# The output stage of a four-layer kernel: bias as a matmul, scale and shift in one ScalarE pass, loads and stores in a new order

## The chip, the core and the metric

The kernel runs on one core of one Trainium2 chip. The time is device microseconds (us) for one execution of the whole program. The engines are PE (TensorE, matmuls), DVE (VectorE), ACT (ScalarE), POOL (GpSimd) and SP (SyncE, which issues DMAs). The change touches the last stage alone, the function `phase_final`.

## The reference

The program is a stack of four layers (a recurrent mixer, a gated expert layer, a rotary attention, and a "sliced" attention), each as `x = x + layernorm(layer(layernorm(x)))` on x of shape (4, 2048, 256). The last stage does the end of the fourth layer. There `attn_out` is the attention's output, `x` the layernormed input of the layer, and each sequence of 2048 tokens is cut in 4 slices of n = 512:

```python
for e in range(e_cnt):                      # 4 slices
    sl = slice(e * n, (e + 1) * n)
    m = d // 2 ** e                         # 256, 128, 64, 32
    xm = attn_out[:, sl, :m]
    out = jnp.einsum('bnm,om->bno', xm, o_w[:m, :m]) + o_b[:m]
    pad = d - m
    if pad:
        out = jnp.pad(out, ((0, 0), (0, 0), (0, pad)))
    outs.append(out + x[:, sl, :])
...
# outside: x = x + _layernorm(that)
```

So slice e projects only the first m = 256 >> e features, adds a bias to them, adds the layer's input over the full width, takes a layernorm of the sum over 256 features, and adds the residual row.

## The kernel before, in words

`phase_final` handles 16 groups g = 4b + e of 512 tokens (b the sequence, e the slice), each as a tile of 128 partitions x 4 rows (j) x 256 features. I call groups with e = 0, 1, 2, 3 groups of **width** 256, 128, 64 and 32. What each engine does for group g:

- SP loads `AT` (attention output, transposed; 512, 256, 128 or 64 KB by width; `load_a`, L2238) into one of 3 buffers and `X` (the residual row, 512 KB; `load_x`, L2247) into one of 4. A load of X(g) waits for `y_done` of group g-4; SP's queue alternates `load_a(g)`, `load_x(g+1)`. A wait stops all that stands behind it in that queue.
- PE multiplies AT by the weights OW into PSUM tile `PA` (L2284): 8 matmuls for width 256, 4 for each other width. Each shows in the trace as two MATMUL records (x16, x8). Two PA buffers; PE waits for `z_done` of group g-2.
- DVE: `add(g)` adds the bias to PA in place (L2324), then makes Z = X * scale + PA for the first m features (L2330, 4 instructions). `stats(g)` takes mean and variance of Z (L2339, L2343). `result(g)` makes the shift NB = -mean * rs (L2350) and then Z = Z * rs + X (L2354, 4 instructions; signal `y_done`).
- POOL turns the variance into rs = (var + eps) ** -0.5 (L2269, L2272) as soon as `stats(g)` is done.
- ACT: `rest(g)` makes Z = X * scale for the features from m up (L2297, e > 0). Then `XO = Z + NB` (L2310, 4 instructions) once `y_done` and `nb_done` of the group are there, and ACT itself issues the 512 KB store (L2313).

DVE runs ahead by one group. Its program order is `add(0) stats(0)`, and then round g = `add(g+1) stats(g+1) result(g)`, for g = 0 to 15. All of this order is written out by hand; nothing is rearranged by a scheduler. ACT's order is `rest(1)`, and then `rest(g+2)`, XO(g), store(g).

Of the kernel before, what the change touches and what calls it, by code (L numbers as in the profile page):

```python
# [2203 lines left out]
def phase_final(nc, ao_d, ow_d, ob_d, scales, x_d, out_d):  # L2204
# [3 lines left out]
    NX, NZ = 4, 3  # L2208
    tag = "fin"
    with ExitStack() as ctx:  # L2210
        m = Mem(nc, ctx, tag)
        AT = [m.sb(f"AT{u}", [P, CC, GT]) for u in range(3)]
        X = [m.sb(f"X{u}", [P, J, D]) for u in range(NX)]
        Z = [m.sb(f"Z{u}", [P, J, D]) for u in range(NZ)]
        XO = [m.sb(f"XO{u}", [P, J, D]) for u in range(2)]
        OW = m.sb("OW", [P, CC, D])
        OB = m.sb("OB", [P, D])
        ST = [m.sb(f"ST{u}", [P, J, 6]) for u in range(2)]
# [17 lines left out]
        @block.sync  # L2236
        def _(sp):
            def load_a(g):  # L2238
                b, e = divmod(g, E4)
                ab = ao_d.rearrange("(b c h) d t -> b (h d) c t", b=B, c=CC)[b]  # L2240
                cs = chunks(e)
                k = cs[0][1]
                wait(sp, a_done, g - 2)
                sp.dma_start(AT[g % 3][0:k, 0:len(cs), :],
                             ab[0:k, 0:len(cs), e * GT:(e + 1) * GT]).then_inc(a_ld[g % 3], 16)

            def load_x(g):  # L2247
# [8 lines left out]
            load_x(1)
            load_x(2)
            for g in range(2, NGR):
                load_a(g)
                if g + 1 < NGR:  # L2260
                    load_x(g + 1)

        @block.gpsimd
        def _(pool):
            nc.gpsimd.memset(nhalf[:, :], -0.5).then_inc(half_set, 1)
            pool.wait_ge(half_set, 1)
            for g in range(NGR):
                wait(pool, var, g + 1)
                nc.gpsimd.tensor_scalar(VE[g % 2][:, :], MV[g % 2][:, :, 1], EPS, None, ALU.add).then_inc(eps, 1)  # L2269
                wait(pool, eps, g + 1)  # L2270
                wait(pool, nb_done, g - 1)
                nc.gpsimd.tensor_tensor(RS[g % 2][:, :], VE[g % 2][:, :], nhalf[:, :], ALU.pow).then_inc(rs, 1)  # L2272

        @block.tensor
        def _(pe):
            pe.wait_ge(ow_ld, 16)
            for g in range(NGR):
                e, u = g % E4, g % 2
                wait(pe, a_ld[g % 3], 16 * (g // 3 + 1))
                wait(pe, z_done, g - 1)  # L2280
                for j in range(J):
                    cs = chunks(e)
                    for c, k in cs:
                        ins = nc.tensor.matmul(PA[u][:, j, 0:D >> e], AT[g % 3][0:k, c, j * P:(j + 1) * P],  # L2284
                                               OW[0:k, c, 0:D >> e], start=(c == 0), stop=(c == len(cs) - 1))
                ins.then_inc(a_done, 1)

        @block.scalar
        def _(act):
# [12 lines left out]
            for g in range(NGR):  # L2302
# [15 lines left out]
        def _(dve):
            def add(g):
                u, mm = g % 2, D >> g % E4  # L2320
                if g == 0:
                    dve.wait_ge(ob_ld, 16)
                wait(dve, a_done, g + 1)
                nc.vector.tensor_tensor(PA[u][:, :, 0:mm], PA[u][:, :, 0:mm],  # L2324
                                        OB[:, 0:mm].unsqueeze(1).to_broadcast([P, J, mm]), ALU.add).then_inc(biased, 1)
                wait(dve, biased, g + 1)
# [19 lines left out]
            def result(g):  # L2346
# [13 lines left out]
            for g in range(NGR):  # L2360
# [3 lines left out]
                result(g)  # L2364
# [87 lines left out]
```

## Time and profile before

| | us |
|---|---|
| median of 3 runs | 5029.73 (5026.91 to 5038.87) |
| the profiled execution | 5029.49, of which span 5027.3 |
| last stage, first DMA issue to the end of the span | 4921.4 to 5027.3, 105.9 |
| DVE's first instruction of the stage to the end | 4931.2 to 5027.3, 96.1 |

The span is the part that the trace covers; 2.2 us of the execution lie around it. All times below count from the span's start. The page's shares of busy time (PE 92%, DVE 84%) are those of the whole program, in which an attention of some thousand us stands out. They say nothing of this stage, which is 2% of the span and is read from windows of its own.

### The profile page before, as it was taken

To read this page: it belongs to the slowest core of one execution; us is meant where nothing else is said; L and a number is where in the kernel's file an instruction comes from. 1 tells how busy PE (TensorE), PEld (TensorE's weight loads), DVE (VectorE), ACT (ScalarE), POOL (GpSimd) and SP (SyncE) were. 2 spreads that over 40 slices of the span, in tenths; PEclk is the share of its full clock that TensorE was granted. 3 is DMA by queue.
4 is the path that set the end of the run, shared out by engine and by line. 5 is a ranking of instruction groups with operands and counts; after the bars stand their busy time and mean duration, and the time that the engine had idled before them with its cause. 6 is when DMAs were issued, how large, how long until landed. Compare 5 with 4: busy or idle time off the path is not lost. (4 is left out here: it accounts for less than half of the span.)

```text
span 5027.3 us, 89365 instructions
## 1 busy us (share of the span) xinstructions
PE 4622.3 (92%) x33659; PEld 2057.7 (41%) x33659; DVE 4207.0 (84%) x5551; ACT 3361.4 (67%) x6016; POOL 1333.6 (27%) x881
## 2 busy tenths in 40 slices
PE   6998775896999999999999999999998889999993
PEld 3333541563333333333333333333334445545532
DVE  6999650787999999999999999999994777777736
ACT  4888110231888888888888888888884426666663
POOL 2333210462000000000000000000001239999992
PEclk9999887996999999999999999999997769999996
DMA  5111569687333333344333333433314831323305
GB/s 188 56 55 42 186 232 394 198 271 159 43 55 50 49 49 49 50 55 55 53 49 49 49 49 54 55 55 49 49 20 153 289 86 46 82 60 79 74 5 170
DMA packets 408176, 479.48 MB, mean 95 GB/s; under 512 B 165056, under 2 KB 311264, under 8 KB 390848
## 3 DMA queue, kind: packets, MB, share of 16 engines
q1 hardware_dynamic: 394464, 455.41, 39.2%
q10 hardware_dynamic: 13280, 18.35, 1.1%
q8 instruction: 265, 4.34, 0.4%
q14 instruction: 167, 1.37, 0.1%
HBM read 315.71 MB, written 155.58 MB: 94 GB/s over the span
## 5 line engine op out<-in xcount | busy, mean ns | idle before, releaser
L763 DVE TENSOR_REDUCE at_NM<-at_MX 128x1 f32<-128x1024 f32 (+1 forms) x3008 | 3066.3, 1049 | 241.1 <-PE at_MX L611 216.2
L715 ACT ACTIVATE at_PB<-at_S 128x512 f32<-128x512 f32 x5056 | 2712.1, 597 | 628.3 <-PE at_S L638 503.7
L611 PE MATMUL at_MX<-at_KT,at_QT 48*128 48x512 f32 (+1 forms) x5056 | 1904.2, 454 | 60.6 <-DMA at_VS<-v 46.0
L638 PE MATMUL at_S<-at_QT,at_KT 50*128 50x512 f32 (+1 forms) x5056 | 1898.6, 441 | 8.4 <-ACT at_PB L715 6.0
L650 PE MATMUL at_AV<-at_PB,at_VS 128*32 128x256 f32 (+1 forms) x18304 | 1555.5, 414 | 0.9 <-ACT at_PB L715 0.9
L638 PEld LDWEIGHTS at_S<-at_QT,at_KT 50*128 50x128 f32 (+1 forms) x5056 | 804.8, 187 | 901.1 <-ACT at_PB L715 824.8
L611 PEld LDWEIGHTS at_MX<-at_KT,at_QT 48*128 48x128 f32 (+1 forms) x5056 | 795.8, 190 | 312.5 <-DVE at_NM L763 209.5
L650 PEld LDWEIGHTS at_AV<-at_PB,at_VS 128*32 128x32 f32 x18304 | 369.8, 108 | 820.9 <-ACT at_PB L715 752.0
L547 POOL CAST at_NMR<-at_NMF 16x128 fp32r<-16x128 f32 x79 | 22.1, 279 | 1837.5 <-ACT at_NMF L727 1837.5
L572 POOL TENSOR_TENSOR at_SUM<-at_SUM,at_PB 128x2048 f32<-128x2048 f32 x90 | 415.0, 4611 | 10.9
L913 PE MATMUL wkv_PQ<-wkv_XT,wkv_WT 128*128 128x512 f32 x768 | 340.5, 600 | 50.8 <-DVE wkv_DL L1036 34.2
L572 POOL TENSOR_TENSOR at_SUM<-at_PB 128x2048 f32<-128x2048 f32 x75 | 352.2, 4699 | 30.6 <-ACT at_PB L715 30.0
L913 PEld LDWEIGHTS wkv_PQ<-wkv_XT,wkv_WT 128*128 128x128 f32 x768 | 144.7, 191 | 246.0 <-issue 194.6
L555 POOL TENSOR_TENSOR at_O<-at_FO,at_REC 128x256 f32<-128x256 f32 x64 | 39.9, 624 | 749.8 <-DVE at_REC L778 749.8
L991 POOL TENSOR_TENSOR wkv_EV<-wkv_E2S,wkv_V 128x1024 f32<-128x1024 f32 x32 | 75.5, 2360 | 311.4 <-DVE wkv_MN L1013 132.6
L1201 PE MATMUL r_PA<-r_OC,r_A 128*128 128x256 f32 x512 | 114.4, 382 | 12.3 <-DMA r_A<-ycat 12.3
L1807 PE MATMUL r_QK<-r_WC,r_XT 128*128 128x512 f32 x256 | 120.3, 594 | 0.7 <-DVE r_WC L1970 0.6
L2139 ACT ACTIVATE rows<-moe_PH 128x1024 f32<-128x1024 f32 x8 | 8.2, 1024 | 162.3 <-PE moe_TP L2181 132.0
L1488 PE MATMUL r_PO<-r_XT,r_WS 128*128 128x512 f32 (+2 forms) x136 | 92.0, 837 | 17.8 <-ACT r_XT L1517 17.8
L1201 PEld LDWEIGHTS r_PA<-r_OC,r_A 128*128 128x128 f32 x512 | 97.1, 192 | 26.7 <-DVE r_OC L1309 13.9
L727 ACT ACTIVATE at_NMF<-at_S 16x128 f32<-16x128 f32 x79 | 21.0, 266 | 120.2 <-PE at_S L629 120.2
L1885 ACT ACTIVATE r_VB<-r_PV,r_RS 128x256 f32<-128x256 f32 x64 | 26.8, 470 | 108.4 <-PE r_PV L1817 65.7
(211 smaller groups left out, 3368.0 us busy)
## 6 DMA issues: line engine op xcount, KB each, us to landing
at_QT<-qk SPq DMA_DIRECT2D x402, 128.0 KB, 5.2
moe_W<-in_w SPq DMA_DIRECT2D x48, 1024.0 KB, 11.4
at_KT<-qk SPq DMA_DIRECT2D x384, 128.0 KB, 6.5
at_VS<-v SPq DMA_DIRECT2D x96, 256.0 KB, 9.0
at_KT<-qk SPq DMA_DIRECT2D x96, 256.0 KB, 6.3
qk<-r_HI SPq DMA_DIRECT2D x36, 512.0 KB, 4.2
qk<-r_LO SPq DMA_DIRECT2D x36, 512.0 KB, 5.2
ycat<-wkv_Y SPq DMA_DIRECT2D x32, 512.0 KB, 2.6
```

The lines of the kernel that those rows point to most:

```text
L555: nc.gpsimd.tensor_tensor(O[s % 2][:, :, :], FO[s % 2][:, :, 0:DH], REC[s % 2][:, :].to_broadcast([P, W // VW, DH]), ALU.mult).then_inc(no ...
L572: nc.gpsimd.tensor_tensor(total[:, :, :], other, PB[:, k:k + NCH, :], ALU.add).then_inc(sum_done, 1)
L611: ins = nc.tensor.matmul(MX[r][:, a, :], q_of(s)[h:h + NQ, b * P:(b + 1) * P], k_of(it, s, b * P // W)[h:h + NQ, (c + a) * W:(c + a + 1) * W],
L638: nc.tensor.matmul(SP_[item(it, s, "score", t)[1]][:, :], k_of(it, s, c)[h:h + NQ + 2, kb * P:(kb + 1) * P], q_of(s)[h:h + NQ + 2, c * W:( ...
L650: ins = nc.tensor.matmul(AV[c * VW:(c + 1) * VW, cols], v_of(it, s, c)[:, kb, :], PB[:, (NCH * kb + c) % NPB, cols], start=first, stop=last)
L715: nc.scalar.activation(PB[:, t % NPB, :], SP_[r][:, :], ACT.Exp, scale=scale).then_inc(exp_done, 1)
L763: nc.vector.tensor_reduce(NM4[:, b, c:c + 1], MX[r][:, :, :].rearrange("p a n -> p (a n)"), AX_X, ALU.max, negate=True).then_inc(ring_got, 1)
L913: ins = nc.tensor.matmul(PQ[q][:, tt * 512:(tt + 1) * 512], WT[:, cc, row:row + P], XT[b % 2][:, cc, t0:t0 + 512], start=(cc == 0), stop=( ...
L991: nc.gpsimd.tensor_tensor(EV[s][:, :], E2S[s][:, :], V[s][:, :], ALU.mult).then_inc(pv, 1)
L1201: ins = nc.tensor.matmul(PA[u][:, j, :], A[u][:, q, j * P:(j + 1) * P], OC[:, q, :], start=(q == 0), stop=(q == NC - 1))
L1488: ins = nc.tensor.matmul(PO[a][:, h, :], WS[0:k, c, lo:lo + P], XT[u][0:k, c, :], start=(c == 0), stop=(c == len(ks) - 1))
L1807: ins = nc.tensor.matmul(QK[j % 2][:, :], XT[u][:, c, j * P:(j + 1) * P], WC[:, c, 0:2 * D], start=(c == 0), stop=(c == CC - 1))
```

## The change

In the last stage only:

- Bias: for widths 128, 64 and 32 PE adds it, by one more matmul for each j with a matrix ONE (row 0 ones, else zeros; two new POOL memsets) against OB. Width 256 keeps the DVE addition. PE now waits for OB's load and for ONE before its first matmul.
- Scale and shift: ACT makes XO = Z * rs + NB in its one pass; it waits for `nb_done`, no longer for `y_done`. DVE's L2354 goes. In its place DVE adds the residual row in one operation, XO = XO + X, 128 x 1024, in a new `result(g)`, which waits for `xo_done` of the group; its end is now `y_done`. The shift instruction stands in a function of its own, `shift(g)`.
- DVE's round g is now `add(g+1) stats(g+1) shift(g) result(g-1)`.
- Loads and stores: AT has 4 buffers, X 5, XO 3. SP issues A and X of groups 0 to 3 (X up to 4) at the start. Then for each g it waits for `y_done` of g and issues store(g), load X(g+5), load A(g+4), in that order. ACT issues no DMA.
- POOL's `RS` now waits for `xo_done` of group g-2, where it waited for `nb_done`.

```diff
-    NX, NZ = 4, 3
+    NA, NX, NZ, NO = 4, 5, 3, 3
...
-                wait(sp, a_done, g - 2)
-                sp.dma_start(AT[g % 3][0:k, 0:len(cs), :],
-                             ab[0:k, 0:len(cs), e * GT:(e + 1) * GT]).then_inc(a_ld[g % 3], 16)
+                wait(sp, a_done, g - NA + 1)
+                sp.dma_start(AT[g % NA][0:k, 0:len(cs), :],
+                             ab[0:k, 0:len(cs), e * GT:(e + 1) * GT]).then_inc(a_ld[g % NA], 16)
...
-            for g in range(2, NGR):
-                load_a(g)
-                if g + 1 < NGR:
-                    load_x(g + 1)
+            load_a(2)
+            load_a(3)
+            load_x(3)
+            load_x(4)
+            for g in range(NGR):
+                wait(sp, y_done, g + 1)
+                sp.dma_start(group(tokens(out_d), g), XO[g % NO][:, :, :]).then_inc(o_st[g % NO], 16)
+                if g + NX < NGR:
+                    load_x(g + NX)
+                if g + NA < NGR:
+                    load_a(g + NA)
+            for u in range(NO):
+                sp.wait_ge(o_st[u], 16 * len(range(u, NGR, NO)))
...
+            nc.gpsimd.memset(ONE[:, :], 0.0).then_inc(one_set, 1)
+            pool.wait_ge(one_set, 1)
+            nc.gpsimd.memset(ONE[0:1, :], 1.0).then_inc(one_set, 1)
...
-                wait(pool, nb_done, g - 1)
+                wait(pool, xo_done, g - 1)
...
+            pe.wait_ge(ob_ld, 16)
+            pe.wait_ge(one_set, 2)
...
-                                               OW[0:k, c, 0:D >> e], start=(c == 0), stop=(c == len(cs) - 1))
+                                               OW[0:k, c, 0:D >> e], start=(c == 0), stop=(e == 0 and c == CC - 1))
+                    if e > 0:
+                        k = cs[0][1]
+                        ins = nc.tensor.matmul(PA[u][:, j, 0:D >> e], ONE[0:k, :], OB[0:k, 0:D >> e],
+                                               start=False, stop=True)
...
-                wait(act, y_done, g + 1)
                 wait(act, nb_done, g + 1)
-                wait(act, o_st[u], 16 * (g // 2))
-                for j in range(J):
-                    ins = nc.scalar.activation(XO[u][:, j, :], Z[g % NZ][:, j, :], ACT.Identity, bias=NB[u][:, j:j + 1])
+                wait(act, o_st[g % NO], 16 * (g // NO))
+                for j in range(J):
+                    ins = nc.scalar.activation(XO[g % NO][:, j, :], Z[g % NZ][:, j, :], ACT.Identity,
+                                               bias=NB[u][:, j:j + 1], scale=RS[u][:, j:j + 1])
                 ins.then_inc(xo_done, 1)
-                wait(act, xo_done, g + 1)
-                act.dma_start(group(tokens(out_d), g), XO[u][:, :, :]).then_inc(o_st[u], 16)
...
-                wait(dve, stat, g + 1)
-                for j in range(J):
-                    ins = nc.vector.scalar_tensor_tensor(out=Z[g % NZ][:, j, :], in0=Z[g % NZ][:, j, :], scalar=RS[u][:, j:j + 1],
-                                                         in1=X[g % NX][:, j, :], op0=ALU.mult, op1=ALU.add)
-                ins.then_inc(y_done, 1)
+
+            def result(g):
+                wait(dve, xo_done, g + 1)
+                nc.vector.tensor_tensor(XO[g % NO][:, :, :], XO[g % NO][:, :, :], X[g % NX][:, :, :],
+                                        ALU.add).then_inc(y_done, 1)
...
-                result(g)
+                shift(g)
+                if g > 0:
+                    result(g - 1)
+            result(NGR - 1)
```

SP's queue in the steady part, before (X of one group, then AT of the group before it; the AT of 128x2x512 is that of a width-256 group):

```order
L2249 DMA fin_X<-x 128x1024
L2244 DMA fin_AT<-ao 64x512
L2249 DMA fin_X<-x 128x1024
L2244 DMA fin_AT<-ao 32x512
L2249 DMA fin_X<-x 128x1024
L2244 DMA fin_AT<-ao 128x2x512
```

The same queue after, from store(0) on:

```order
L2265 DMA out<-fin_XO 128x4x256
L2250 DMA fin_X<-x 128x1024
L2245 DMA fin_AT<-ao 128x2x512
L2265 DMA out<-fin_XO 128x4x256
L2250 DMA fin_X<-x 128x1024
L2245 DMA fin_AT<-ao 128x512
```

A store has moved in ahead of each pair of loads, and all three of a triple stand behind one wait for `y_done`.

DVE before, the round that ends at the bias addition of width-256 group 4 (its first row is Z of group 3, `fin_PA` with 128x1024 is group 4):

```order
L2330 SCALAR_TENSOR_TENSOR fin_Z<-fin_X,scales,fin_PA 128x32 x4
L2339 BN_STATS fin_ST<-fin_Z 128x6 x4
L2343 BN_AGGR fin_MV<-fin_ST 128x2 x4
L2350 SCALAR_TENSOR_TENSOR fin_NB<-fin_MV,fin_RS 128x4
L2354 SCALAR_TENSOR_TENSOR fin_Z<-fin_Z,fin_RS,fin_X 128x256 x4
L2324 TENSOR_TENSOR fin_PA<-fin_PA,fin_OB 128x1024
```

DVE after, from Z of group 2 to the same place (L2370 with `fin_XO` is the residual addition, first that of group 0, then that of group 1):

```order
L2345 SCALAR_TENSOR_TENSOR fin_Z<-fin_X,scales,fin_PA 128x64 x4
L2354 BN_STATS fin_ST<-fin_Z 128x6 x4
L2358 BN_AGGR fin_MV<-fin_ST 128x2 x4
L2365 SCALAR_TENSOR_TENSOR fin_NB<-fin_MV,fin_RS 128x4
L2370 TENSOR_TENSOR fin_XO<-fin_XO,fin_X 128x1024
L2345 SCALAR_TENSOR_TENSOR fin_Z<-fin_X,scales,fin_PA 128x32 x4
L2354 BN_STATS fin_ST<-fin_Z 128x6 x4
L2358 BN_AGGR fin_MV<-fin_ST 128x2 x4
L2365 SCALAR_TENSOR_TENSOR fin_NB<-fin_MV,fin_RS 128x4
L2370 TENSOR_TENSOR fin_XO<-fin_XO,fin_X 128x1024
L2339 TENSOR_TENSOR fin_PA<-fin_PA,fin_OB 128x1024
```

The instruction that signals `y_done` of a group has moved one round further down: group 0's now stands after the statistics of group 2, where it stood after those of group 1.

## Rows read from the trace of the kernel before

**Rows 1.** Busy time by window: one cycle of four groups; us, busy us by engine (records), clock, DMA.

```profile
4951.50:4974.90 23.40, 9.65 (x42) 8.22 (x41) 20.41 (x72) 12.12 (x32) 6.24 (x8) 0.64 0.72 239
```

**Rows 2.** Waits, 4918 to 5027: who waited for whom, us in total, times, longest.

```profile
PE fin_PA L2284 <- DMA fin_AT<-ao: 48.7, 8, 10.6
...
DVE fin_PA L2324 <- PE fin_PA L2284: 20.3, 4, 13.8
```

**Rows 3.** Timeline: start us, length us, engine, line, work; in brackets idle time and releaser.

```profile
4951.51 1.23 DVE L2324 TENSOR_TENSOR fin_PA<-fin_PA,fin_OB 128x1024 f32<-128x1024 f32 x1 [1.12 <-PE fin_PA L2284]
...
4957.83 0.69 DVE L2324 TENSOR_TENSOR fin_PA<-fin_PA,fin_OB 128x512 f32<-128x512 f32 x1
...
4958.56 1.12 DVE L2330 SCALAR_TENSOR_TENSOR fin_Z<-fin_X,scales,fin_PA 128x128 f32<-128x128 f32 x4
...
4961.50 1.67 DVE L2354 SCALAR_TENSOR_TENSOR fin_Z<-fin_Z,fin_RS,fin_X 128x256 f32<-128x256 f32 x4
...
4961.60 1.91 PE L2284 MATMUL fin_PA<-fin_OW,fin_AT 32*128 32x32 f32 x8 [5.95 <-DMA fin_AT<-ao]
...
4963.08 0.43 DVE L2324 TENSOR_TENSOR fin_PA<-fin_PA,fin_OB 128x256 f32<-128x256 f32 x1
4963.20 0.33 SPq L2249 DMA_DIRECT2D fin_X<-x  x1
...
4963.55 0.86 DVE L2330 SCALAR_TENSOR_TENSOR fin_Z<-fin_X,scales,fin_PA 128x64 f32<-128x64 f32 x4
4963.57 0.43 SPq L2244 DMA_DIRECT2D fin_AT<-ao  x1
...
4968.13 0.72 DVE L2330 SCALAR_TENSOR_TENSOR fin_Z<-fin_X,scales,fin_PA 128x32 f32<-128x32 f32 x4
...
4969.09 6.67 PE L2284 MATMUL fin_PA<-fin_OW,fin_AT 128*128 128x256 f32 x24 [5.58 <-DMA fin_AT<-ao]
...
4970.67 1.67 DVE L2354 SCALAR_TENSOR_TENSOR fin_Z<-fin_Z,fin_RS,fin_X 128x256 f32<-128x256 f32 x4
...
4974.90 1.23 DVE L2324 TENSOR_TENSOR fin_PA<-fin_PA,fin_OB 128x1024 f32<-128x1024 f32 x1 [2.57 <-PE fin_PA L2284]
```

**Rows 4.** Chain that ended last, shortest and longest of four width-256 PE blocks: start, us.

```profile
4925.92 5.18 PE fin_PA L2284 x16
...
4992.46 6.05 PE fin_PA L2284 x16
```

**Rows 5.** DMAs issued at 4922.4, 4941.6, 4958.3, 4963.2, 4963.6: KB, us from issue to landing.

```profile
fin_OB<-in_o_b SPq DMA_DIRECT2D x1, 128.0 KB, 5.6
...
fin_AT<-ao SPq DMA_DIRECT2D x1, 512.0 KB, 4.5
...
fin_AT<-ao SPq DMA_DIRECT2D x1, 64.0 KB, 3.3
...
fin_X<-x SPq DMA_DIRECT2D x1, 512.0 KB, 3.4
...
fin_AT<-ao SPq DMA_DIRECT2D x1, 512.0 KB, 5.5
```

**Rows 6.** PE alone by window: us, busy us (records), granted clock (1.00 is 2.4 GHz), DMA.

```profile
4961.60:4963.50 1.90, 1.90 (x8) 0.50 0.46 162
4977.90:4979.10 1.20, 1.07 (x8) 1.00 0.00 0
```

**Rows 7.** Groups of instructions, whole program: a 128x1024 addition with all operands in SBUF.

```profile
L1067 DVE TENSOR_TENSOR wkv_PD<-wkv_PD,wkv_ER 128x1024 f32<-128x1024 f32 x32 | 39.0, 1219 | 1.6 <-ACT wkv_PD L971 1.6
```

**Rows 8.** Timeline of the stage's end, same columns as rows 3.

```profile
5017.35 0.38 DVE L2343 BATCH_NORM_AGGREGATE fin_MV<-fin_ST 128x2 f32<-128x6 f32 x4
...
5018.34 1.12 POOL L2272 TENSOR_TENSOR fin_RS<-fin_VE,fin_nhalf 128x4 f32<-128x4 f32 x1
...
5021.63 1.70 ACT L2310 ACTIVATE fin_XO<-fin_Z,fin_NB 128x256 f32<-128x256 f32 x4 [0.53 <-DVE fin_Z L2354]
5023.36 0.38 ACTq L2313 DMA_DIRECT2D out<-fin_XO  x1
```

More of the change, by code:

```diff
@@ L2211, in phase_final @@
         m = Mem(nc, ctx, tag)
-        AT = [m.sb(f"AT{u}", [P, CC, GT]) for u in range(3)]
+        AT = [m.sb(f"AT{u}", [P, CC, GT]) for u in range(NA)]
         X = [m.sb(f"X{u}", [P, J, D]) for u in range(NX)]
         Z = [m.sb(f"Z{u}", [P, J, D]) for u in range(NZ)]
-        XO = [m.sb(f"XO{u}", [P, J, D]) for u in range(2)]
+        XO = [m.sb(f"XO{u}", [P, J, D]) for u in range(NO)]
         OW = m.sb("OW", [P, CC, D])
         OB = m.sb("OB", [P, D])
+        ONE = m.sb("ONE", [P, P])
         ST = [m.sb(f"ST{u}", [P, J, 6]) for u in range(2)]
@@ L2223, in phase_final @@
         PA = [m.ps(f"PA{u}", [P, J, D]) for u in range(2)]
-        ow_ld, ob_ld, half_set, a_done, biased, z_done, rest_done, stat, var, eps, rs, y_done, nb_done, xo_done = (
-            m.sem(n) for n in ("ow_ld", "ob_ld", "half_set", "a_done", "biased", "z_done", "rest_done", "stat", "var",
+        ow_ld, ob_ld, half_set, one_set, a_done, biased, z_done, rest_done, stat, var, eps, rs, y_done, nb_done, xo_done = (
+            m.sem(n) for n in ("ow_ld", "ob_ld", "half_set", "one_set", "a_done", "biased", "z_done", "rest_done", "stat", "var",
                                "eps", "rs", "y_done", "nb_done", "xo_done"))
         x_ld = [m.sem(f"x_ld{u}") for u in range(NX)]
-        a_ld = [m.sem(f"a_ld{u}") for u in range(3)]
-        o_st = [m.sem(f"o_st{u}") for u in range(2)]
+        a_ld = [m.sem(f"a_ld{u}") for u in range(NA)]
+        o_st = [m.sem(f"o_st{u}") for u in range(NO)]
         block = ctx.enter_context(nc.Block())
@@ L2276, in _ @@
             pe.wait_ge(ow_ld, 16)
+            pe.wait_ge(ob_ld, 16)
+            pe.wait_ge(one_set, 2)
             for g in range(NGR):
                 e, u = g % E4, g % 2
-                wait(pe, a_ld[g % 3], 16 * (g // 3 + 1))
+                wait(pe, a_ld[g % NA], 16 * (g // NA + 1))
                 wait(pe, z_done, g - 1)
@@ L2283, in _ @@
                     for c, k in cs:
-                        ins = nc.tensor.matmul(PA[u][:, j, 0:D >> e], AT[g % 3][0:k, c, j * P:(j + 1) * P],
-                                               OW[0:k, c, 0:D >> e], start=(c == 0), stop=(c == len(cs) - 1))
+                        ins = nc.tensor.matmul(PA[u][:, j, 0:D >> e], AT[g % NA][0:k, c, j * P:(j + 1) * P],
+                                               OW[0:k, c, 0:D >> e], start=(c == 0), stop=(e == 0 and c == CC - 1))
[3 more added lines that the diff above has]
+                                               start=False, stop=True)
                 ins.then_inc(a_done, 1)
@@ L2320, in add @@
                 u, mm = g % 2, D >> g % E4
-                if g == 0:
+                wait(dve, a_done, g + 1)
+                if mm == D:
                     dve.wait_ge(ob_ld, 16)
[L2323 to L2326, printed above, removed]
+                    nc.vector.tensor_tensor(PA[u][:, :, :], PA[u][:, :, :], OB[:, :].unsqueeze(1).to_broadcast([P, J, D]),
+                                            ALU.add).then_inc(biased, 1)
+                    wait(dve, biased, g // E4 + 1)
                 wait(dve, x_ld[g % NX], 16 * (g // NX + 1))
@@ L2344, in stats, with shift @@
                 ins.then_inc(var, 1)
-            def result(g):
+            def shift(g):
                 u = g % 2
```

2 lines of the change are left out of this document (removed).

## The prediction

> **What bounds the stage now.** I read the window of one full cycle of four groups first [rows 1]. From one width-256 bias addition to the next pass 23.40 us; DVE is busy 20.41 of them, ACT 12.12, PE 9.65, and the DMA engines 0.72 of the time at 239 GB/s. So DVE is the bound, with a remainder of about 3 us a cycle. The waits say what the remainder is: DVE waited 20.3 us for PE in four waits, the longest 13.8 being the start of the stage, so 6.5 in the other three; and PE had waited for loads of AT [rows 2]. The timeline shows one such place: AT of group 8 (width 256) is issued at 4963.57, PE starts at 4969.09, DVE idles 2.57 us until 4974.90 [rows 3]. PE, ACT and POOL idle elsewhere without cost. Of this, DVE's own work is what the change takes away; the chain "load of AT, PE, DVE" is what it moves.
>
> **DVE's work per group, before.** Start to start in [rows 3]: width 256 takes 4957.83 - 4951.51 = 6.3 us; width 128 takes 4963.08 - 4957.83 = 5.25, of which the bias addition 4958.56 - 4957.83 = 0.73; width 64 from its Z on, without the bias, is about 4.25 (the width-128 one is 4963.08 - 4958.56 = 4.5, and its four narrower Z instructions save 0.26: 1.12 against 0.86); width 32 without bias is 4970.67 - 4968.13 = 2.54, plus the L2354 block. That block occupies 4963.08 - 4961.50 = 1.58 us.
>
> **DVE's work after.** Three bias additions of four go. L2354 (1.58) goes, and one 128x1024 addition comes: 1.22 us in the row where all operands lie in SBUF [rows 7]; with the gap for its wait I take 1.25, so 0.33 saved a group. A round then is 6.0, 4.2, 3.9 and 3.8 us for widths 256, 128, 64, 32, in sum 17.9 against 23.4 with the wait or 20.7 without. ACT's pass with scale as well as bias has no row of this stage; between no change (1.70 for four [rows 8]) and double it, it stays hidden: it starts at `shift(g)` and is needed one round later, 3.8 us at the least. Cost nothing; were that cover gone, 1.7 a group. The stores' 0.38 us of issue leave ACT, which has slack. DMA bytes do not change: at 239 / 0.72 = 332 GB/s, the cycle's 5 MB need 15 us, under 17.9.
>
> **The start.** PE began at 4925.92 and took 5.18 [rows 4]. It now waits for OB too, issued at 4922.4 with 5.6 us to land [rows 5]: 4928.0, so 2.1 us later. ONE's two memsets are done by then. DVE's first instruction is at 4928.0 + 5.2 + 0.1 = 4933.3.
>
> **When is AT issued now?** This is the step that decides. A(g+4) is issued after `y_done` of g, behind store(g) and X(g+5). But `result(g)` has moved one round down, so between the end of result(0) and the bias addition of group 4 lies one round, that of group 3: 3.8 us. Before, A(g+4) was also issued at `y_done` of g (X is ahead of it in SP's queue), but that stood two rounds ahead. "Four groups ahead" by number is one round ahead in time.
>
> What must fit in that round, for width 256: the landing. A fixed part of a DMA, from a lone 512 KB: 3.4 us [rows 5] less 0.524 MB / 332 GB/s = 1.6 leaves 1.8. Store, X and A are 1.57 MB, 4.7 us, so 6.5, plus 0.1 for the semaphore: A lands 6.6 us after `y_done`. Below, it could be 5.3: X issue to A landed was 0.37 + 4.5 = 4.9 once [rows 3, 5], plus 0.4 for the store's issue if its bytes don't hold A back. Above, 7.5: the other row (0.37 + 5.5) plus 1.6 for the store. I take 6.6, between them, because the store is first in the same queue. Then PE, 5.18 to 6.05 [rows 4]; I take 5.6. Sum 6.6 + 5.6 + 0.1 = **12.3** us after `y_done`, against 3.8 of cover: DVE idles 8.5.
>
> The rows show that a load behind another in SP's queue lands later (64 KB behind X 3.3, 512 KB behind X 4.5 and 5.5 [rows 5]). The Trainium skill, page "DMA: Bandwidth & Descriptors", section "Queues, rings and completion order", says that each DMA engine consumes one issuer's descriptors in ring order and takes turns between issuers; that speaks against moving stores into SP's queue. By that rule A lands at 6.6; if the store's bytes took their turn behind it, at 5.3, and each cycle would be 1.3 us shorter.
>
> **Width 64.** A(g+4) of width 64 is issued at the end of the width-256 round and has one width-128 round, 4.2 us. Store, X and 128 KB are 1.18 MB: 3.6 + 1.8 = 5.4 us. PE now runs 8 matmuls, 16 records. PE was at full clock for 8 records in 1.07 us when it had just worked, and at 0.50 (1.2 GHz) for 8 records in 1.90 after idling 5.95 us in wait for a load [rows 3, 6]. So 16 records cost 2.1 or 3.8. Here PE has idled some 9 us (its blocks for groups 8 and 9 end about 2 us into the cycle, the AT lands at 11.4), so I take 3.8: 5.4 + 3.8 = 9.2, DVE idles 5.0 us. The Trainium skill, page "TensorE: Matmul & The Clock Gate", section "What's actually happening", says that the throttled state is the default and activity releases it; by it the block starts slow, 3.8, and without it the cycle would be 1.7 shorter. For widths 128 and 32 the extra matmuls hide: their AT was issued before the long wait, and PE does them while DVE works on the group before.
>
> **The sum.** A cycle from the width-256 addition: 6.0; 4.2; then the width-64 addition at 6.0 + 9.2 = 15.2; 3.9 on, at 19.1, `y_done` releases the next width-256 load (and width 32 starts: its AT came at 10.2 + 5.4 = 15.6, PE 2.1 to 3.8, not late by more than 0.3); next cycle at 19.1 + 12.3 = **31.4** against 23.4. First cycle: 4933.3 + 4.7 (group 0 without L2354) + 3.0 (group 1 without a result) + 3.9 = 4944.9 is result(0)'s end; group 4 starts at 4957.2, where it was at 4951.51. Two cycles: 5020.0 for group 12. Group 15 starts 19.1 later, 5039.1; its statistics end 2.6 later, 5041.7. The tail: before, 5017.73 to 5027.3, 9.6 us. After: POOL 1.73, shift 0.2, ACT 1.75, addition 1.3, store 5023.36 to 5027.3 = 3.9, in all 9.0 [rows 8]. Span 5050.7, plus 2.2 around it: **5053 us**, 23 over the profiled 5029.5, which is the median (5029.7) to 0.3 us. Most of it is the 8.0 a cycle: waits of 13.5 in place of 2.6, less 2.8 of DVE work saved.
>
> **Rivals.**
> - *The same mechanism at its low ends* (landing 5.3, PE 5.2, width 64: 4.1 + 0.1 + 2.1 = 6.3). The cycle is 6.0 + 6.3 + 3.9 + 10.6 = 26.8; group 4 at 4955.5, group 12 at 5009.1, group 15 at 5025.3, end 5036.9: 5039 us, within 0.3% of before. For it: one landing row. Against it: all ends must come together. At the high ends (7.5 + 6.05 + 0.05; width 64: 10.1) the cycle is 33.6 and the time 5059.5.
> - *DVE stays the bound* and the change gains: each AT is there in time. Then after 4944.9 come 3.8, two cycles of 17.9, and 14.1 to group 15 at 4998.6; 5001.2, end 5010.2: 5012 us, 17 faster. It needs landing and PE together within 3.8 us of `y_done`, where PE alone took 5.18 [rows 4]; or loads that don't wait for `y_done` of their triple, which the queue rules out.
> - *A wait in ACT's queue*: `rest(g+2)` stands ahead of XO(g) and waits for X(g+2), and XO(g) for store(g-3). X(g+2) is issued two rounds and a statistic ahead, over 8 us, and lands in about 5; with `rest` (1.5) and XO (1.7) it just fits. If X took 8 us, result would be late about 2 us in narrow rounds, say 10 over the stage: 5063.
>
> **How the numbers follow.** Forecast as summed, any size between 5045 and 5060: 0.73. Low ends, 5038 to 5045: 0.14; a part of the low ends and a mild clock, still within 0.3%: 0.04. DVE-bound, faster: 0.04. ACT's wait or more: 0.05. A measurement of this kernel can tell about 0.3% from no change, 15 us: slower means over 5044.8. Slower 0.78, same 0.18, faster 0.04. Range 5038 to 5062, from the low ends to just over the high ends.
>
> **What would show it.** In the new profile: PE's first matmul near 4928; DVE idle of about 8.5 us before each of three width-256 additions and about 5 before width-64 Z of groups 6, 10, 14, with PE as the releaser and the AT load ahead of it; cycles of 31; DVE busy 17 to 18 a cycle; ACT's L2328 at about 0.5 us each. Wrong would be: waits under 4 us before width 256, width-64 blocks at full clock (2.1), or a DVE addition of XO far from 1.22.

## The result

The changed kernel takes 5057.8 us in the median of 5 runs (5052.1 to 5068.9), the kernel before 5030.4 in the median of 5 (5026.9 to 5038.9). The ratio is 1.0051, 95% interval 1.0037 to 1.0065: slower by half a per cent. The forecast was 5053 with a range of 5038 to 5062.

The stage's length from its first DMA issue to the end of the span was 105.9 us before. Here the issue is at 4934.00, so it is 5067.0 - 4934.0 = **133.0 us**, 27.1 more, close to the difference of the medians (27.3). The point at which the stage starts wanders between executions by far more than the changes under study: 4913.8 to 4940.3 in all kernels below, whose earlier stages are the same code. So I compare stage lengths, not spans. A second profiled execution of the changed kernel gave 5057.2 - 4924.4 = 132.8.

First, one full cycle of four groups, from one width-256 bias addition to the next; the columns are those of [rows 1]:

```profile
4971.04:5002.30 31.26, 14.28 (x65) 12.97 (x64) 17.27 (x57) 12.66 (x28) 8.85 (x8) 0.62 0.50 166
```

DVE is busy 17.27 us of 31.3, where it was 20.41 of 23.4: the work was taken off as meant, and DVE is no longer the bound. The DMA engines' share falls from 0.72 to 0.50. PE's busy time rises from 9.65 to 14.28. What all of them wait for stands in the waits of the stage, answering to [rows 2]:

```profile
ACT fin_XO L2328 <- DVE fin_NB L2365: 63.0, 15, 11.4
...
PE fin_PA L2299 <- DMA fin_AT<-ao: 53.0, 6, 10.6
DVE fin_PA L2339 <- PE fin_PA L2299: 43.9, 4, 16.9
...
DVE fin_Z L2345 <- PE fin_PA L2303: 16.6, 3, 6.0
PE fin_PA L2299 <- DMA fin_OB<-in_o_b: 12.6, 1, 12.6
```

The longest of DVE's four waits of L2339 is the start (16.9); 27.0 lie in the other three, 9 each, where before these three had 6.5 in all. L2345 adds 16.6 in three waits, which the kernel before did not have: these are the width-64 groups, whose first instruction is now the Z instruction. The last row is PE's wait before its first matmul of the stage, which the load of OB now ends. The timeline around groups 6 to 8 answers to [rows 3]:

```profile
4977.02 0.39 SPq L2265 DMA_DIRECT2D out<-fin_XO  x1
...
4977.46 0.50 SPq L2250 DMA_DIRECT2D fin_X<-x  x1
4978.01 0.97 SPq L2245 DMA_DIRECT2D fin_AT<-ao  x1
...
4982.62 0.69 PE L2299 MATMUL fin_PA<-fin_OW,fin_AT 64*128 64x64 f32 x2 [9.84 <-DMA fin_AT<-ao]
...
4985.67 0.63 PE L2303 MATMUL fin_PA<-fin_OB,fin_ONE 64*128 64x64 f32 x2
...
4986.34 0.85 DVE L2345 SCALAR_TENSOR_TENSOR fin_Z<-fin_X,scales,fin_PA 128x64 f32<-128x64 f32 x4 [5.27 <-PE fin_PA L2303]
...
4989.01 1.22 DVE L2370 TENSOR_TENSOR fin_XO<-fin_XO,fin_X 128x1024 f32<-128x1024 f32 x1
...
4990.14 0.71 DVE L2345 SCALAR_TENSOR_TENSOR fin_Z<-fin_X,scales,fin_PA 128x32 f32<-128x32 f32 x4
4990.25 0.39 SPq L2265 DMA_DIRECT2D out<-fin_XO  x1
...
4990.69 0.50 SPq L2250 DMA_DIRECT2D fin_X<-x  x1
...
4991.24 0.95 SPq L2245 DMA_DIRECT2D fin_AT<-ao  x1
...
4992.67 1.22 DVE L2370 TENSOR_TENSOR fin_XO<-fin_XO,fin_X 128x1024 f32<-128x1024 f32 x1
...
4996.99 5.63 PE L2299 MATMUL fin_PA<-fin_OW,fin_AT 128*128 128x256 f32 x18 [7.14 <-DMA fin_AT<-ao]
...
5002.43 1.23 DVE L2339 TENSOR_TENSOR fin_PA<-fin_PA,fin_OB 128x1024 f32<-128x1024 f32 x1 [8.54 <-PE fin_PA L2299]
```

Read it from the store of group 2, issued at 4977.02: X(7) and A(6) stand behind it, and AT of group 6 (width 64) is issued at 4978.01, late because `y_done` of group 2 is. PE starts group 6 at 4982.62, 5.6 us after the store's issue, and is done at 4986.3; DVE has idled 5.27 us. From 4989.01 to 4990.23 DVE makes result(4) (L2370): this releases store(4) at 4990.25, X(9) and A(8), issued at 4991.24. Between this and the place where DVE needs group 8 (width 256) there is one DVE round, that of group 7, from 4990.14 to 4993.9. PE starts group 8 at 4996.99, 6.7 us after the store's issue, and DVE at 5002.43, after 8.54 us of idleness.

PE's clock answers to [rows 6]. The windows are the width-64 block, the start and the end of the width-256 block:

```profile
4982.62:4986.20 3.58, 3.58 (x16) 0.50 0.77 255
4996.99:4998.99 2.00, 2.00 (x5) 0.50 1.04 399
5000.40:5002.40 2.00, 2.00 (x11) 0.99 0.00 0
```

The columns are as in [rows 6]. After 9.84 us without work the 16 records of the width-64 block take 3.6 us, all at 0.50.

### The profile page after: what moved, and what is told of

It is laid out like the page before. It is cut to its first block and busy times, and to the rows that moved or that the text cites. A ratio compares the mean times of both kernels' runs of the same rounds, so it can differ in the third digit from the quotient of the medians.

```text
span 5067.0 us, 89500 instructions
## 1 busy us (share of the span) xinstructions
PE 4653.8 (92%) x33755; PEld 2082.5 (41%) x33755; DVE 4195.5 (83%) x5491; ACT 3368.5 (66%) x6016; POOL 1341.5 (26%) x883
## 5 line engine op out<-in xcount | busy, mean ns | idle before, releaser
L1201 PE MATMUL r_PA<-r_OC,r_A 128*128 128x256 f32 x512 | 117.6, 390 | 12.3 <-DMA r_A<-ycat 12.3
L2139 ACT ACTIVATE rows<-moe_PH 128x1024 f32<-128x1024 f32 x8 | 8.2, 1024 | 163.0 <-PE moe_TP L2181 131.9
L2299 PE MATMUL fin_PA<-fin_OW,fin_AT 128*128 128x256 f32 (+3 forms) x160 | 48.9, 436 | 67.8 <-DMA fin_AT<-ao 53.0
## 6 DMA issues: line engine op xcount, KB each, us to landing
moe_W<-in_w SPq DMA_DIRECT2D x48, 1024.0 KB, 11.9
```

The lines of the kernel that those rows point to most:

```text
L1201: ins = nc.tensor.matmul(PA[u][:, j, :], A[u][:, q, j * P:(j + 1) * P], OC[:, q, :], start=(q == 0), stop=(q == NC - 1))
L2299: ins = nc.tensor.matmul(PA[u][:, j, 0:D >> e], AT[g % NA][0:k, c, j * P:(j + 1) * P], OW[0:k, c, 0:D >> e], start=(c == 0), stop=(e == 0 ...
```

## The experiments

Each kernel is the changed kernel, or the one before, with the edit shown. "Stage" is always from the stage's first DMA issue to the end of the span, from one profiled execution. Of the experiments only e1 and e6 were timed more often and have an interval; the others stand on one execution, and the two kernels that were profiled twice agree with themselves to 0.3 us.

| kernel | stage | cycle(s) between width-256 additions |
|---|---|---|
| before | 105.9 | 23.4, 23.6 |
| changed | 133.0 and 132.8 | 31.4, 33.0 |
| e1, AT load ahead of the wait | 103.1 | 21.9, 25.6 |
| e2, store last | 121.7 | 28.1, 27.9 |
| e3 / e11, bias by DVE | 129.3 / 129.6 | 30.5, 30.7 / 31.1, 31.3 |
| e4, result in its own round | 125.5 | 27.1, 28.1 |
| e5, before with bias by PE | 105.5 | 21.6, 23.2 |
| e6, AT 8 ahead | 87.6 | 17.4, 17.4 |
| e7, the same, bias by DVE | 93.1 | 18.9, 18.9 |
| e8, before with AT 6 ahead | 99.9 | 20.7, 20.7 |
| e9, OB waited for later | 133.0 | 31.4, 32.9 |

### e1: release a round earlier

```diff
             for g in range(NGR):
+                if g + NA < NGR:
+                    load_a(g + NA)
                 wait(sp, y_done, g + 1)
                 sp.dma_start(group(tokens(out_d), g), XO[g % NO][:, :, :]).then_inc(o_st[g % NO], 16)
                 if g + NX < NGR:
                     load_x(g + NX)
-                if g + NA < NGR:
-                    load_a(g + NA)
```

> The changed kernel with one edit: in SP's loop load A(g+4) stands ahead of the wait for y_done of g, so it is released one round earlier (by y_done of g-1). Stage means the last stage, from its first DMA issue to the end of the span: 105.9 us before, 133.0 changed; cycles from one width-256 addition to the next are 31.4 and 33.1 in the changed kernel. Late-release theory (AT is released one DVE round before it is needed): with two rounds of cover, 7.7 us, against 12.5 needed, the wait before width 256 falls from 9 to about 4.8, that before width 64 goes, cycles of 22.5 to 23, group 4 starts 8.5 us earlier, stage about 101, time about 5025. Queue-order rival (the store ahead of the load is what costs): store and X are still ahead of the load, so nothing changes, stage about 133. PE-block rival (the doubled narrow matmul blocks cost it): stage 125 or more.

Measured: stage 103.1, and 5026.1 us in the median of 10 runs against 5033.2 of 13 of the kernel before, ratio 0.9987 (0.9977 to 0.9996). Each load but the first still has a store and an X ahead of it in the queue; it merely belongs to the `y_done` of the group before. The waits are these:

```profile
DVE fin_PA L2339 <- PE fin_PA L2299: 26.3, 4, 16.2
...
DVE fin_Z L2345 <- PE fin_PA L2303: 4.1, 3, 1.7
```

Of the 43.9 us, 26.3 are left, 16.2 of them the start; the 16.6 of width 64 are gone, and 4.1 has come for width 32, whose PE block now is the late one. The late-release theory gets its 30 us (133.0 to 103.1, 101 expected); the queue-order rival and the PE-block rival fall as explanations of the whole. The three waits before width 256 were 0.83, 2.81 and 6.39 us, in sum 10.0, the last more than expected. AT of group 12 was issued at 4980.49 and took 7.8 us to land, where that of group 8, issued at 4958.80 in the same place of its cycle, took 5.4; PE began it at 4988.28, and its block took 6.8 us, the first 6 of them at a granted clock of 0.50. The windows of those 6 us show the DMA engines busy all the time (the last two columns are their share and GB/s):

```profile
4981.00:4983.00 2.00, 1.72 (x8) 1.72 (x9) 1.97 (x9) 1.94 (x5) 0.81 (x1) 0.50 0.97 281
4983.00:4985.00 2.00, 1.90 (x9) 1.77 (x9) 0.34 (x2) 1.62 (x4) 1.41 (x2) 0.50 1.00 347
4985.00:4987.00 2.00, 0.00 (x0) 0.00 (x0) 1.97 (x8) 0.00 (x0) 0.00 (x0) 0.50 1.07 379
```

So once the release is early, what is left is partly a backlog on the DMA engines. That the bytes ahead of this load made its landing late was not tried by a kernel of its own.

### e2: same release, store behind the loads

```diff
                 wait(sp, y_done, g + 1)
-                sp.dma_start(group(tokens(out_d), g), XO[g % NO][:, :, :]).then_inc(o_st[g % NO], 16)
-                if g + NX < NGR:
-                    load_x(g + NX)
                 if g + NA < NGR:
                     load_a(g + NA)
+                if g + NX < NGR:
+                    load_x(g + NX)
+                sp.dma_start(group(tokens(out_d), g), XO[g % NO][:, :, :]).then_inc(o_st[g % NO], 16)
```

> The changed kernel with one edit: after each wait for y_done SP issues load A(g+4), load X(g+5), store(g), in that order; the release is as late as before. Queue-order effect alone: A lands about 4.0 us after y_done instead of 6.6 for width 256 and 3.2 instead of 5.4 for width 64; waits of 6.3 and 3; cycles of about 27.4; stage about 119. If the queue takes the transfers in turn and not in order, A lands as late as now and the stage stays at 132 to 133. If queue order were the whole loss, stage about 106.

Measured: stage 121.7, 11 less than the changed kernel and 3 more than expected; waits before width 256 of 8.0, 7.2 and 6.6 us, before width 64 of 3.3 to 3.7. So the order within the triple is a real part, about 2 us per wait, and the lateness of the triple as a whole is the larger part.

The traces split these 2 us. In the changed kernel AT of width 256 is issued 1.0 us after the store and lands 5.6 to 5.7 us after its own issue; here it is issued first and lands after 5.0 to 5.1. So 1.0 us is the earlier issue, and only some 0.6 the bytes of store and X. For width 64 (128 KB) the landing falls from 4.6 to 5.0 us to 3.6 to 3.9. The 4.0 us that were expected for width 256 did not come, though nothing stood ahead of the load. These are the windows behind its issue at 4973.06 (the last two columns are the DMA engines' share and GB/s):

```profile
4974.06:4975.06 1.00, 0.00 (x0) 0.00 (x0) 1.00 (x4) 0.00 (x0) 0.18 (x1) 0.50 0.84 193
4975.06:4976.06 1.00, 0.00 (x0) 0.00 (x0) 0.96 (x7) 0.46 (x1) 0.45 (x1) 0.50 0.87 137
4976.06:4977.06 1.00, 0.00 (x0) 0.00 (x0) 0.64 (x1) 1.00 (x3) 0.92 (x2) 0.50 0.82 186
4977.06:4978.06 1.00, 0.00 (x0) 0.00 (x0) 0.00 (x0) 0.62 (x2) 0.83 (x1) 0.50 0.98 374
```

The first three move 0.516 MB, as much as the AT load has (0.524), at 137 to 193 GB/s with the engines busy 0.82 to 0.87 of the time; the rate rises to 374 only behind them. AT landed at 4978.2, X at 4979.5 and the store at 4980.8, in the order of their issue. That agrees with the ring-order rule that the prediction took from the Trainium skill, page "DMA: Bandwidth & Descriptors", section "Queues, rings and completion order". No run moves the stores back to ACT's queue, so what that part of the change costs by itself is not shown.

### e3 and e11: the bias by DVE again

The edit takes out the ONE matmuls and PE's waits for OB and ONE, and puts the DVE addition back for every width:

```diff
-                    if e > 0:
-                        k = cs[0][1]
-                        ins = nc.tensor.matmul(PA[u][:, j, 0:D >> e], ONE[0:k, :], OB[0:k, 0:D >> e],
-                                               start=False, stop=True)
...
-                if mm == D:
-                    dve.wait_ge(ob_ld, 16)
-                    nc.vector.tensor_tensor(PA[u][:, :, :], PA[u][:, :, :], OB[:, :].unsqueeze(1).to_broadcast([P, J, D]),
+                nc.vector.tensor_tensor(PA[u][:, :, 0:mm], PA[u][:, :, 0:mm],
+                                        OB[:, 0:mm].unsqueeze(1).to_broadcast([P, J, mm]), ALU.add).then_inc(biased, 1)
```

> The changed kernel with the bias of all widths added by DVE again, as in the kernel before (PE no longer waits for OB and ONE; no extra matmuls). Late-release theory: the width-64 PE block falls from 3.8 to 1.9 us, DVE gains 1.45 us of work a cycle, the start is 2 us earlier: waits of about 8.5 (width 256) and 2.4 (width 64), cycles of about 30.2, stage about 126. PE-block rival: the loss is mostly here, stage 106 to 112.

> The changed kernel with the bias of all widths by DVE, once more: in the first execution group 0's AT took 5.5 us to land and its PE block 6.36, and the stage was 129.3 where 126 was expected. If that was the start's chance, the stage is 126 to 128 and the waits before widths 256 and 64 are again 8.2 and 2.4; if 129 comes again, the PE bias costs 4 us in the changed kernel and no more.

Measured: 129.3, then 129.6. So in the changed kernel the PE bias costs 3.5 us net: with the doubled width-64 block DVE waits 16.6 us before these groups in sum, without it 9.4 and 9.6, and this difference alone is more than the work that DVE is spared (busy 17.27 us a cycle against 18.70, some 5.7 us over the stage). It is not the cause of the 27. The expectation of 126 was some 3.5 too low. The waits before width 256 were 8.20, 8.24 and 8.18 us (9.40, 8.69 and 8.63 in the second execution), and those before width 64, with the old four matmuls of PE, 2.8 to 3.5 where 2.4 was expected. The start differs between the two (DVE's first instruction 12.5 and 10.5 us after the stage's first issue), and the stages hardly do, since the waits of the one with the early start are longer.

### e4: result back in its own round

```diff
                 shift(g)
-                if g > 0:
-                    result(g - 1)
-            result(NGR - 1)
+                result(g)
```

> The changed kernel with result(g) put back in round g, right behind shift(g): DVE then waits for ACT's pass (about 2.2 us) in every round, but y_done comes a round earlier. Late-release theory: DVE's work and waits for ACT are 26.7 us a cycle, AT of width 256 has two rounds, 12.1 us, of the 12.5 it needs, no wait before width 64: cycles of about 27.2, stage about 125, 8 less than the changed kernel in spite of 16 added waits. If the release were not the cause, the added waits come on top: cycles of 40, stage about 160.

```profile
DVE fin_XO L2370 <- ACT fin_XO L2328: 34.3, 16, 2.1
DVE fin_PA L2339 <- PE fin_PA L2299: 19.9, 4, 16.9
```

The waits of e4's stage, above, show that this kernel adds 34.3 us of waits for ACT to DVE, 2.1 in each of 16 rounds, and still is 7.5 us shorter than the changed kernel: 125.5, as expected to half a us. Three of the four waits for PE shrink to 0.6 to 1.7 us, and those before width 64 are gone, because `y_done` comes a round sooner. Together with e1 this shows the cause from both sides: with the load ahead of the wait, or the signal a round sooner, most of the waits for AT go.

### e5: the PE bias alone on the kernel before

The edit is the `ONE` part of the diff, with the DVE additions of the narrow widths taken out, on the kernel before.

> The kernel before with one part of the change alone: the bias of widths 128, 64 and 32 by PE (ONE, and PE's wait for OB). DVE works 1.45 us less a cycle, but AT of width 256 keeps its landing, so about 0.8 of that comes back as wait; the start is 1 to 3 us later. Late-release theory (AT is released as in the kernel before): cycles of 22.6 to 23, stage (first DMA issue of the last stage to the end) 104 to 107, against 105.9 before. PE-block rival: the doubled blocks cost on their own, stage over 112.

Measured: 105.5. DVE's waits before width 256 were 3.1, 2.3 and 3.9 us, where the kernel before had 1.1, 2.6 and 2.8. The three waits grew by 2.8 us in sum. DVE's busy time fell from 20.41 to 18.98 us a cycle, and the cycles from 23.4 and 23.6 to 21.6 and 23.2, so half of the saving was lost to waits for AT and half stayed: from DVE's first instruction to the end the stage took 92.8 us, 3.3 less than the 96.1 before. The start took that back. DVE's first instruction came 12.8 us after the stage's first issue, against 9.8: PE, now waiting for OB, began 1.5 us later, and its first block took 6.8 us in place of 5.3.

### e6, e7, e8: AT far ahead

e6 is the changed kernel with these edits:

```diff
-    NA, NX, NZ, NO = 4, 5, 3, 3
+    NA, NX, NZ, NO = 8, 5, 3, 3
...
             load_x(3)
+            load_a(4)
+            load_a(5)
             load_x(4)
+            load_a(6)
+            load_a(7)
             for g in range(NGR):
+                if g + NA < NGR:
+                    load_a(g + NA)
                 wait(sp, y_done, g + 1)
...
-                if g + NA < NGR:
-                    load_a(g + NA)
...
-            pe.wait_ge(ob_ld, 16)
-            pe.wait_ge(one_set, 2)
...
+                if g == 1:
+                    pe.wait_ge(ob_ld, 16)
+                    pe.wait_ge(one_set, 2)
```

> The changed kernel with AT in 8 buffers, its loads ahead of the waits for y_done (released by PE's use of the buffer, behind the previous triple), and PE waiting for OB and ONE only ahead of group 1. Late-release theory: no wait of DVE for PE is left after the start; cycles of 17.9 to 19, stage about 90, time about 5015, 15 us under the kernel before. If the DMA engines are the next limit (5 MB a cycle at 332 GB/s is 15 us), cycles of 19 to 21 with waits on X, stage 92 to 98.

The two cycles by window, columns as in [rows 1]:

```profile
4942.36:4959.78 17.42, 13.78 (x69) 12.29 (x68) 17.11 (x58) 11.89 (x28) 8.19 (x8) 0.71 0.85 274
4959.78:4977.19 17.41, 13.53 (x68) 12.05 (x67) 17.10 (x59) 12.59 (x30) 8.85 (x9) 0.71 0.85 273
```

And of the waits of the stage the one of DVE for PE (L2344 and L2304 are L2339 and L2299 of the changed kernel, five lines further down):

```profile
DVE fin_PA L2344 <- PE fin_PA L2304: 15.4, 2, 14.8
```

Stage 87.6, cycles of 17.4, DVE busy throughout: after the start (14.8) this row has 0.6 us left. The time is 5004.9 us (median of 6) against 5031.6 (median of 11), ratio 0.9952 (0.9937 to 0.9966). This is the fastest version, 0.5% under the kernel before. The DMA engines are busy 0.85 of the time, at 274 GB/s, and did not become the limit.

e7 is the same with the bias of all widths by DVE:

> As the kernel with AT in 8 buffers, but with the bias of all widths by DVE, so that PE's blocks are short. If DVE is the bound there, its 1.45 us of work come back in each cycle: stage 5 to 6 us longer than that one, about 95. If PE's doubled blocks were still on the path, the stage would be the same or shorter.

Measured: 93.1, 5.5 more. So the PE bias is worth 5.5 us once DVE is the bound (and PE's wait for OB is out of the way), and costs 3.5 where AT is late: the sign of that part hangs on the loads.

e8 is the kernel before with only its AT loads further ahead:

```diff
-                wait(sp, a_done, g - 2)
-                sp.dma_start(AT[g % 3][0:k, 0:len(cs), :],
-                             ab[0:k, 0:len(cs), e * GT:(e + 1) * GT]).then_inc(a_ld[g % 3], 16)
+                wait(sp, a_done, g - 5)
+                sp.dma_start(AT[g % 6][0:k, 0:len(cs), :],
+                             ab[0:k, 0:len(cs), e * GT:(e + 1) * GT]).then_inc(a_ld[g % 6], 16)
...
-            for g in range(2, NGR):
-                load_a(g)
-                if g + 1 < NGR:
-                    load_x(g + 1)
+            load_a(2)
+            load_x(3)
+            load_a(3)
+            load_a(4)
+            load_a(5)
+            for g in range(4, NGR):
+                if g + 2 < NGR:
+                    load_a(g + 2)
+                load_x(g)
```

> The kernel before with AT in 6 buffers and A(g+2) issued ahead of X(g), nothing else changed. The three waits for PE ahead of the later width-256 additions (1.1, 2.6, 2.8 us) go: cycles of 20.8, stage about 99.4, time about 5023. It tells how much of the gain of the deep kernel is the loads alone and how much the work taken from DVE.

Measured: 99.9, cycles of 20.7. The loads alone are worth 6.0 us (one execution each), and the other parts of the change a further 12.3 (99.9 to 87.6) once the loads are early.

### e9 and e10: the start, and the spread

e9 moves PE's wait for OB and ONE, as in e6, and nothing else. e10 is the changed kernel again.

> The changed kernel with one edit: PE waits for OB and ONE ahead of group 1 only, not ahead of its first matmul. By the prediction's term for the start, group 0's bias addition comes 2.1 us earlier after the stage's first DMA issue (about 10.7 instead of 12.8 in the changed kernel), and the stage is about 131. AT of group 0 has landed 3.9 to 5.5 us after issue in the runs so far; where it is 5.5, only 0.5 is gained and the wait for OB was hidden by it.

> The changed kernel as it is, for the spread of the stage between executions. If the profiled stage is typical: 131 to 135 us, cycles of 31 to 33, with differences from PE's granted clock and the landings. The place where the stage starts may differ by 10 us and more (4934.0 in the first profile, 4913.8 to 4931.6 in the others).

Measured: e9 133.0, where 131 was expected, and e10 132.8, so the wait for OB costs nothing that shows in the stage. DVE's first instruction came 12.5 us after the stage's first issue in e9, 12.4 in e10, 12.8 in the first profile. PE itself did start earlier in e9, 5.7 us after that issue against 6.2 and 6.4, but AT of group 0 took 5.1 us to land, and the first PE block took 6.8 us against 6.2 and 6.4. The spread of the stage between two executions of one kernel is a few tenths in the two pairs on record.

## Why the prediction was right, point by point

- **What bounds, and where the work goes**: as written. L2370 took 1.219 us (1.22 taken), DVE's busy time is 17.27 a cycle. The rounds were: width 256 from 4971.04 to 4976.92, 5.9 (6.0); width 128 from 4976.92 to 4981.07, 4.15 (4.2); width 64 3.8 (3.9).
- **The release**, the step that decides: shown by e1 and e4. From the end of result(0) (4958.30) to group 4's addition (4971.04) it took 12.7 us; 12.3 was the sum. PE began at 4964.93, 6.6 after, as summed; the PE block took 6.1, not 5.6.
- **The landing** came out right, 6.6 to 6.8 us each time, but not by the working given, and in this the forecast had luck. The working was 1.8 us fixed and 4.7 for the 1.57 MB of store, X and AT at 332 GB/s. By it an AT load with nothing ahead would land after 3.4 us, and e2 shows 5.0 to 5.1 (at the stage's start it took 3.9 to 5.5). The bytes ahead were priced too high (some 0.6 us by e2, where 1.05 MB at 332 GB/s give 3.2). The AT load itself, which moved at 137 to 193 GB/s in e2, was priced too low, and its issue 1.0 us after the store had no term. These errors cancelled.
- **Cycles**: 31.39 where 31.4 was forecast, but 33.05 for the next; e10 had 31.35 and 33.04, e9 31.43 and 32.92. So the second cycle is longer by 1.5 to 1.7 each time. Two terms were too small. The width-64 load: I let it land 5.4 us after `y_done`; PE began 5.6 us after it in the first cycle, but 6.3 in the second (5014.73 after 5008.39). And the wide PE block, 5.4 us in the first cycle and 6.5 in the second: its granted clock rose from 0.50 to 1.00 some 3.4 us after its start in the first and 5.5 in the second. Of the 0.7 us in the load, 0.3 is a later issue: in this triple AT was issued 1.27 us after the store, in all the other triples 0.98 or 0.99:

```profile
5008.42 0.39 SPq L2265 DMA_DIRECT2D out<-fin_XO  x1
5008.85 0.51 SPq L2250 DMA_DIRECT2D fin_X<-x  x1
5009.69 0.66 SPq L2245 DMA_DIRECT2D fin_AT<-ao  x1
```

  The other 0.4 is the landing, 5.0 us from issue in place of 4.6. The same late issue stands at the same group in e3, e9 and e10 (1.29, 1.28 and 1.29 us); why there is not known.
- **Width 64 at the low clock**: right, 3.6 to 3.8 us for 16 records, granted 0.50. PE had been idle 9.8, 10.6 and 9.9 us before these blocks (9 was taken). The waits were 5.27, 5.98 and 5.29 (5.0).
- **The start**: the term was right, and a second one was missed. PE's first matmul was forecast 6.6 us after the stage's first issue, 2.1 later than before. It came after 6.4, 1.9 later, and the trace names the load of OB as what ended its wait; AT of group 0 had landed 1.0 us before. The six kernels whose PE waits for OB at once all show OB as the releaser and PE's start 6.0 to 7.2 us after the first issue; the seven others show it after 4.5 to 6.1. What I did not have is the PE block behind it: 6.4 us from PE's first matmul to DVE's first instruction, where it was 5.3. The windows of PE alone, columns as in [rows 6], first the kernel before and then the changed one, show the granted clock at 0.50 for 3.0 us before and for 5.4 here:

```profile
4925.92:4928.92 3.00, 3.00 (x7) 0.50 0.85 304
4928.92:4931.10 2.18, 2.18 (x12) 1.00 1.03 422
...
4940.41:4945.80 5.39, 5.39 (x13) 0.50 1.05 361
4945.80:4946.79 0.99, 0.99 (x7) 0.99 0.98 381
```

  Over all kernels this first block took 5.1 to 6.8 us, so DVE's first instruction came 9.8 us after the first issue (before) to 12.9 (e4). What makes the clock rise sooner in one execution than in another stays open. In e9, without the wait, PE starts only 0.4 to 0.7 us earlier than in the changed kernel, because AT landed later than before, and the longer block takes it back.
- **The tail**: 9.0 was forecast (its terms add up to 8.9) and 9.8 came (5057.18 to 5067.0), 9.6 before. Two terms: ACT's pass of four with scale and bias took 2.08, not 1.70; and POOL's L2282 took 1.18 where L2269 had taken 0.44. The end of the timeline, answering to [rows 8], shows both:

```profile
5057.27 1.18 POOL L2282 TENSOR_SCALAR fin_VE<-fin_MV 128x4 f32<-128x4 f32 x1 [1.37 <-DVE fin_MV L2358]
...
5058.53 1.03 POOL L2285 TENSOR_TENSOR fin_RS<-fin_VE,fin_nhalf 128x4 f32<-128x4 f32 x1
5059.59 0.16 DVE L2365 SCALAR_TENSOR_TENSOR fin_NB<-fin_MV,fin_RS 128x4 f32<-128x4 f32 x1 [1.23 <-POOL fin_RS L2285]
...
5059.79 2.08 ACT L2328 ACTIVATE fin_XO<-fin_Z,fin_NB,fin_RS 128x256 f32<-128x256 f32 x4 [0.45 <-DVE fin_NB L2365]
5061.90 1.23 DVE L2370 TENSOR_TENSOR fin_XO<-fin_XO,fin_X 128x1024 f32<-128x1024 f32 x1 [1.01 <-ACT fin_XO L2328]
```

- **The rivals**: "DVE stays the bound" is what e6 does with the loads moved, and its 17.4 a cycle and stage of 87.6 us answer to the 17.9 and the stage of 88.8 (5010.2 less 4921.4) given for it. "Low ends" did not come. "A wait in ACT's queue" did not decide: XO(g) ended ahead of need, and DVE waited 1.0 us for it in all, at the end.
- **The size**: a stage of 129.3 was forecast, 133.0 measured. Of the 3.7 us, the start has 0.95 (DVE's first instruction 12.8 us after the first issue, 11.9 forecast), the PE block of group 4 0.3, the second cycle 1.65 (a width-64 load 0.7 later and a wide PE block 1.1 longer than in the first, 0.1 less elsewhere), and the tail 0.8.

## What to carry to other kernels

Count how far ahead a load is in the rounds of the engine that signals its release, not in buffers: a fourth buffer did not bring the load forward here, because it stood behind the wait for a result that had itself been put off by a round. When a step is put off in a software pipeline, look at every queue that waits for its signal, and take loads that don't need that signal out from behind it. And price a saving on an engine only after asking what arrives last: with the bias on PE the stage was 0.4 us shorter, 3.5 us longer or 5.5 us shorter in three settings of the loads, and in the first of them a later start hid most of what it gave.

## What was not expected of the hardware

ACT's L2328 with a per-partition scale beside the per-partition bias took 589 ns in the mean, L2310 with the bias alone 496: 93 ns for the operand. The Trainium skill, page "ScalarE: Activation LUTs", section "What ACT_TABLE_LOAD costs", says that each such pointer operand adds about 93 ns; the traces agree. The groups by line and form, whole stage (busy us, mean ns | idle time before and its releaser):

```profile
L2328 ACT ACTIVATE fin_XO<-fin_Z,fin_NB,fin_RS 128x256 f32<-128x256 f32 x64 | 33.2, 589 | 63.0 <-DVE fin_NB L2365 63.0
...
L2370 DVE TENSOR_TENSOR fin_XO<-fin_XO,fin_X 128x1024 f32<-128x1024 f32 x16 | 19.5, 1219 | 1.0 <-ACT fin_XO L2328 1.0
L2282 POOL TENSOR_SCALAR fin_VE<-fin_MV 128x4 f32<-128x4 f32 x16 | 17.0, 1060 | 90.2 <-DVE fin_MV L2358 90.2
```

The same view of the kernel before, where the two operations stand at L2310 and L2269:

```profile
L2310 ACT ACTIVATE fin_XO<-fin_Z,fin_NB 128x256 f32<-128x256 f32 x64 | 27.3, 496 | 40.9 <-DVE fin_Z L2354 40.9
...
L2269 POOL TENSOR_SCALAR fin_VE<-fin_MV 128x4 f32<-128x4 f32 x16 | 6.8, 425 | 72.0 <-DVE fin_NB L2350 55.2 <-DVE fin_MV L2343 16.8
```

POOL's 128x4 operation went from 425 to 1060 ns in the mean without any change to it. The timeline of the changed kernel shows two of them, and that of the kernel before (L2269) the one that is short there:

```profile
4954.54 0.23 POOL L2282 TENSOR_SCALAR fin_VE<-fin_MV 128x4 f32<-128x4 f32 x1 [1.43 <-DVE fin_MV L2358]
...
4957.08 1.22 DVE L2370 TENSOR_TENSOR fin_XO<-fin_XO,fin_X 128x1024 f32<-128x1024 f32 x1
4957.21 1.18 POOL L2282 TENSOR_SCALAR fin_VE<-fin_MV 128x4 f32<-128x4 f32 x1 [1.33 <-DVE fin_MV L2358]
...
4958.22 0.71 DVE L2345 SCALAR_TENSOR_TENSOR fin_Z<-fin_X,scales,fin_PA 128x32 f32<-128x32 f32 x4
...
4936.14 0.23 POOL L2269 TENSOR_SCALAR fin_VE<-fin_MV 128x4 f32<-128x4 f32 x1 [14.61 <-DVE fin_MV L2343]
```

The one at 4957.21 starts 0.13 us after DVE's L2370, whose two inputs both lie in SBUF, and ends 0.09 us after it. So do all fourteen that start beside an L2370 in the changed kernel, with 1.18 us each; the two that start beside other DVE work, of which 4954.54 is one, take 0.23. In the kernel before, fifteen start beside the first of L2354's four instructions, which also read two inputs in SBUF but last 0.48 us each, and take 0.44; the one that does not takes 0.23. The Trainium skill, page "SBUF — State Buffer", section "Who interferes with whom", says that a DVE instruction with two SBUF inputs and a GpSimd instruction that reads SBUF exclude each other; these traces agree. It cost something only in the tail, where nothing covers POOL: 0.7 us. No run was made to take the two apart there.
